# Self-attention in a decoder layer: the order of two DMA transposes in SyncE's queue

## The reference

```
q, k, v = x @ wq, x @ wk, x @ wv          # per head, 128 wide
qn, kn  = rms_norm(q) * q_scale, rms_norm(k) * k_scale
attn    = softmax(einsum('bqhd,bkhd->bhqk', qn, kn))
out     = einsum('bhqk,bkhd->bqhd', attn, v)
x       = x + einsum('bqhd,hde->bqe', out, wo)
```

## Time and profile before

| | us |
|---|---|
| median of 3 runs (lowest, highest) | 2565.74 (2563.83, 2566.78) |
| the profiled execution, its own time | 2562.61 |
| its span, first to last instruction | 2560.1 |
| PE busy in the span | 2459.1 |
| DVE, ACT, POOL busy | 1554.3, 1340.1, 844.0 |
| DMA transposes issued by SP | 252 |

### The profile page before, as it was taken

One profiled execution on the slowest core, in us unless ns is written; L12 is line 12 of the kernel. 1 busy time (PEld: TensorE's weight loads), 2 busy tenths in 40 slices (PEclk: granted clock), 3 DMA queues, 4 the chain that ended last, 5 costly groups with the idle time before them and its releaser, 6 DMA issues.

```text
span 2560.1 us, 46046 instructions
## 1 busy us (share of the span) xinstructions
PE 2459.1 (96%) x16474; PEld 1334.5 (52%) x16474; DVE 1554.3 (61%) x3592; ACT 1340.1 (52%) x4109; POOL 844.0 (33%) x794
## 2 busy tenths in 40 slices
PE   6998999999999999999888999999999999999998
PEld 3554554554554555544454465465465465465466
DVE  7777766666566666666545655655655655655644
ACT  4554555555555555565464563563563563564433
POOL 3333333333333333333222422422422422422412
PEclk9999999999999999999969999999999999999999
DMA  5677667777677767798611001001001001001000
GB/s 157 147 175 164 148 151 166 157 166 167 144 164 169 156 154 179 163 187 186 145 63 50 33 18 53 1 18 53 1 18 53 1 17 53 1 18 41 8 17 14
DMA packets 456259, 241.56 MB, mean 94 GB/s; under 512 B 389136, under 2 KB 391824, under 8 KB 455284
## 3 DMA queue, kind: packets, MB, share of 16 engines
q1 hardware_dynamic: 456034, 238.63, 39.8%
HBM read 78.66 MB, written 32.77 MB: 44 GB/s over the span
## 4 chain that ended last, share of the span: by engine, by line
PE 90%; DVE 4%; ACT 3%; issue 2%; POOL 1%; POOLq 0%; ACTq 0%; DVEq 0%
PE ps L1553 25%; PE ps L1555 24%; PE ps L1554 24%; PE ps L1732 3%; PE ps L1733 2%; PE ps L1734 2%; PE ps L1846 2%; ACT mem L974 2%; PE ps L1830 1%; PE ps L1802 1%; PE ps L1742 1%; PE ps L1746 1%; PE ps L1744 1%; PE ps L1824 1%; DVE mem L1224 1%
## 5 line engine op out<-in xcount | busy, mean ns | idle before, releaser
L1553 PE MATMUL ps<-mem 128*128 128x512 f16 (+7 forms) x3992 | 1226.8, 326 | 46.0 <-issue 30.3
L1554 PE MATMUL ps<-mem 128*128 128x512 f16 (+7 forms) x3992 | 1238.2, 325 | 0.0
L1555 PE MATMUL ps<-mem 128*128 128x512 f16 (+7 forms) x3992 | 1222.2, 325 | 0.0
L1553 PEld LDWEIGHTS ps<-mem 128*128 128x128 f16 (+3 forms) x3992 | 413.5, 104 | 372.4 <-issue 51.2
L1555 PEld LDWEIGHTS ps<-mem 128*128 128x128 f16 (+3 forms) x3992 | 414.7, 104 | 316.7 <-issue 9.0
L1554 PEld LDWEIGHTS ps<-mem 128*128 128x128 f16 (+3 forms) x3992 | 416.4, 104 | 305.0 <-issue 8.0
L749 POOL TENSOR_TENSOR mem<-mem 128x500 f32<-128x500 f32 (+1 forms) x231 | 269.2, 1165 | 460.6 <-DVE mem L1505 194.6
L699 POOL TENSOR_TENSOR mem<-mem 128x8 f32<-128x8 f32 x100 | 163.7, 1637 | 510.1 <-DVE mem L1137 510.1
L844 ACT ACTIVATE mem<-ps,mem 100x100 f32<-100x100 f32 x512 | 169.1, 346 | 186.4 <-DVE mem L1167 185.4
L1505 DVE TENSOR_TENSOR mem<-mem 128x500 f16<-128x500 f32 (+1 forms) x231 | 144.7, 650 | 177.0 <-ACT mem L1032 170.8
L711 POOL TENSOR_TENSOR mem<-mem 100x400 f16<-100x400 f32 x128 | 158.5, 1238 | 184.6 <-ACT mem L854 184.6
(11 more groups left out here) (123 smaller groups left out, 3045.5 us busy)
## 6 DMA issues: line engine op xcount, KB each, us to landing
x<-mem SPq DMA_DIRECT2D x100, 256.0 KB, 2.9
mem<-x SPq DMA_DIRECT2D x75, 256.0 KB, 3.7
mem<-in_x SPq DMA_DIRECT2D x50, 256.0 KB, 3.3
mem<-x SPq DMA_DIRECT2D x12, 1000.0 KB
mem<-mem SPq DMA_DIRECT2D x32, 200.0 KB
mem<-mem SPq DMA_DIRECT2D x6, 1000.0 KB
out<-mem SPq DMA_DIRECT2D x6, 1000.0 KB
mem<-in_wq SPq DMA_DIRECT2D x16, 256.0 KB, 4.1
```

The source lines that it names most:

```text
L1553: pe.matmul(out_ap, ah, bh, start=(i == 0), stop=False)
L1554: pe.matmul(out_ap, ah, bl, start=False, stop=False)
L1555: mm = pe.matmul(out_ap, al, bh, start=False, stop=(i == len(pairs) - 1))
```

## The change

In SP's loop over the steps the two calls change places: a step's tiles are turned first, and the probabilities of batch n + 1 after them. Nothing else differs: the same DMAs with the same waits, on the same queue.

```
                     load_rows(yn, rows_of(x1, 0, GB), GB, "yn_in")
                     load_keys(keys_of(0, GB), GB)
+                for u in projected_at(n - 1):
+                    turn_tile(u)
                 if 0 <= n + 1 < STEPS:
                     turn_probs(n + 1)
-                for u in projected_at(n - 1):
-                    turn_tile(u)
```

## The result

The changed kernel takes 2545.51 us (median of 4 runs, 2543.38 to 2549.29) where the kernel before takes 2566.26 (4 runs, 2563.83 to 2566.81): a ratio of 0.9929, 95% interval 0.9913 to 0.9944. That is 20.7 us less; forecast were 16.5 less, 2549.2. The two profiled executions of the changed kernel took 2549.29 and 2551.17 us, with spans of 2546.9 and 2549.4.

A forecast was written before the change was run, and what follows sets the result against it. PE bounds most of stage A, so only its 17.6 us idle could be won: 14.8 from waits plus 1.7 from clock, 16.5 us; 2562.6 became 2546.1, plus 3.1 gave 2549.2 us. Range 2543 to 2554, chance 0.70.

The forecast's parts named there:

- Step (1): On SP's queue, the tile issues at least 1.4 us earlier, and its landing moves by as much.
- the floor of 1.4: Least saving per tile in us: the other transpose's issue with its waits and small gaps; 1.43 in the step shown.
- rival A: The tile's transfer, not its issue, is the limit: gain only 9 us, time 2556 to 2557; chance 0.13.
- Step (2): Of PE's 15 waits before scores, 310 to 1240 us, eleven vanish and two leave 0.7 and 1.8: 14.8 us saved.
- Step (3): PE's waits before 310 and at 1248.44 us count at nothing; upper bound 6.8 us.
- Step (4): The granted clock, 0.91 between 1140 and 1160 us, no longer falls: 1.7 us more, between 0 and 1.8.
- (5): The probabilities leave later, behind a tile's issue of 4.24 or 5.65 us, but their cover suffices: cost 0.
- (6): SP's queue has the same work and reaches later DMAs earlier; its wait for `qlo` holds up nothing that could have gone.
- rival C: Probabilities become late behind the tile's transfer and hold ACT, kernel slower: 2575 us; chance 0.04.
- The offset: The 3.1 us by which before's median exceeded its profiled execution, added to 2546.1 to give 2549.2.
- Rival B: DVE and ACT chains are late next; if all is given back, 2563 to 2566 us, no change; chance 0.08.
- rival D: Waits outside the stretch and the 2.5 us forecast to stay also go: up to 26 us, 2540; chance 0.05.

The follow-up runs named there:

- e1: The changed kernel run once more with no edit, for a second profile: 2547.14 us, ratio 0.9943 to the kernel before.
- e3: Against the kernel before, only the 24 tiles turned twice go ahead of the probabilities, the others stay behind: 2552.75 us, ratio 0.9961.
- e4: Against the kernel before, only the 76 tiles turned once go ahead of the probabilities, double turns stay behind: 2559.64 us, ratio 0.9985.
- e7: Changed kernel, but of a double turn only the copy into the fifth slot precedes the probabilities, the other half follows, with its own semaphore: 2541.68 us, ratio 0.9910.
- e11: The kernel of e7 run once more, with no further edit: 2542.49 us, ratio 0.9914 to the kernel before.
- e2: Changed kernel, but SP again waits for `plo` and `o` before it turns a step's tile: 2554.49 us, ratio 0.9968 to the kernel before.
- e8: Changed kernel, but probabilities are turned behind `place_values`, the store and the residual rows of the next step: 2551.99 us, ratio 0.9951.
- e5: Changed kernel, but tiles are turned ahead of the store, residual rows and all loads, behind `place_values`: 2569.02 us, ratio 1.0016 to the kernel before.
- e6: Changed kernel, but tiles are turned before everything else of the step, `place_values` too: 2651.04 us, ratio 1.0344 to the kernel before.

## Why the prediction was right, and where it was not

**The mechanism: shown.** PE's waits for turned queries and keys were the only idle time of the stretch that mattered. Each ends 0.09 us after a tile's landing, and they shrank with the order (e1), by tile (e3, e4), and by halving the double turn (e7, e11).

**Step (1), "the landing moves by as much as the issue does": nearly right on the average, wrong where it mattered, by 1.05 us at the wait near 632.** Over the tiles turned between 310 and 1240 the issue comes 2.4 us earlier on the average after DVE L1162 has ended (0.4 us after it, before 2.8), and the landing 2.1 us earlier. So the issue gained more than the floor of 1.4, and most of that reached the landing. At the five tiles whose waits stayed the issue gained 1.35, 1.37, 1.36, 1.45 and 2.17 us, as forecast, and the landing only 0.30, 0.62, 0.70, 0.72 and 1.48. Two of them, as SP and PE have them in the changed kernel:

```profile
1135.65 4.94 SPq L583 DMA_TRANSPOSE mem<-mem  x1
...
1142.76 0.22 PE L1553 MATMUL ps<-mem 128*100 128x100 f16 x1 [2.42 <-issue]
...
1190.86 4.67 SPq L583 DMA_TRANSPOSE mem<-mem  x2
...
1199.40 0.22 PE L1553 MATMUL ps<-mem 128*100 128x100 f16 x1 [0.70 <-issue]
```

From issue to PE's start 7.11 and 8.54 us, where it was 1153.69 - 1147.32 = 6.37 and 1213.51 - 1205.65 = 7.86. Over the whole stretch the issue of L583 went from a middle of 2.23 us to 2.54, its landing from 4.5 to 4.8. This is rival A, at these tiles and not in general. Where SP comes to the tile at most 0.3 us after the end of its DMA before, which is so at 21 of 78 tiles, the first issue takes 3.3 us and its landing 5.6 on the average; where SP had stood waiting for more than 1 us, at 51, they take 2.2 and 4.8. That in the old order the tile's way was freer, by the time that SP had spent waiting and issuing the other transpose, fits this but is not shown: the transfers ahead and the length of the issue moved together, and no run separates them.

**Step (2), the sum.** Forecast to stay: 0.7 + 1.8 = 2.5 us at two waits. Measured: 6.1 at five, 1.89, 0.44, 0.65, 2.42 and 0.70. So 11.2 us of listed idle time went, not 14.8. The floor of 1.4 us was one for the issue, but not for the landing: two of the eleven short waits, 1.06 and 1.35 us, stayed in part.

**A term that was missing.** The listed idle time is too small. In the changed kernel the matmul at 629.94 is drawn 0.38 us long, but matmuls of this kind follow each other every 0.21 or 0.22 us (629.73, 629.94). The scores could have begun at 630.16, so the loss is 2.05 us, not the 1.89 in the brackets. By this a wait costs 0.16 us more than it shows; ten waits fewer make 1.6 us, an estimate from this one place. That pays for nearly half of the error in (2). With the 1.8 us of the clock, 11.2 + 1.6 + 1.8 = 14.6 us, and stage A of the first profile is 14.1 us shorter (1259.88 - 1245.78).

**Step (3), the waits outside count nothing: right,** to 0.2 us at each of the three places shown.

**Step (4), the clock: right in one profile and wrong in the other.** The granted clock between 1140 and 1160 was 1.00 in the first profile of the changed kernel:

```profile
1140.00:1160.00 20.00, 17.58 (x111) 8.74 (x110) 10.75 (x25) 9.73 (x31) 5.55 (x5) 1.00 1.03 224
```

and 0.91 in the second, with the same 2.4 us of wait. The threshold that I read from two rows (2.19 kept it, 3.30 did not) does not exist as such: in the second profile 2.1 us lowered it, and in e2's 2.35 us lowered it (0.91 from 620 to 640) while 2.75 us did not (1.00 from 1140 to 1160).

**Steps (5) and (6), the probabilities and SP's queue: right for the change itself.** The probabilities have a wide cover (e8). Behind SP's new waits at `klo` and `qlo` lay less cover than (6) made it seem: one place further ahead they held up loads and values (e5, e6). The landing of L602 kept its middle, 3.4 before and 3.3 us after. The Trainium skill, DMA: Bandwidth & Descriptors, section Queues, rings and completion order, has each DMA engine take descriptors in ring order. The trace agrees as far as it goes: for all 100 tiles the probabilities of the same step landed after the tile issued ahead of them, by 0.6 us at least, though their later issue alone may give that. And issued behind the tile, they landed as soon after their own issue as before; rival C did not come about.

**The offset.** I added 3.1 us because the median of before lay above its profiled execution. For the changed kernel it lies 3.8 us below. In the two profiled executions the gain is 2562.61 - 2549.29 = 13.3 us, in the medians 20.7 and, run again, 15.9. That 16.5 lies between them is in part luck: the sum of (2) was 3.6 us too large, a term was missing, and the offset had no ground. That the time fell 3.7 us beside 2549.2 owes as much to this as to any step. Rival B (something else late next) took nothing that is seen beside the 1.2 us at stage A's end; rival D would have needed the outer waits.

## What to carry to other kernels

In an in-order issue queue, rank the DMAs by how long after issue each is wanted, and read that margin from the trace for every one of them, the plain loads too: here some of the tiles had none, the probabilities most of a step, and values and weights so little that a further move cost 22 to 104 us. Look at the engine's waits too: what stands behind a wait is late by it. Where one DMA that is wanted early is two transfers, give the half that is wanted first a semaphore of its own. And count a wait from start to start of the matmuls around it, not only by the idle time that the profile lists.

## What was not expected of the hardware

One DMA transpose of 128 x 2048 two-byte elements held SP for 1.70 to 4.24 us before and 1.70 to 4.94 after, though nothing in its form differs. It took longer where SP came straight from another DMA (3.3 us against 2.2, see step (1)); why, no run shows. Issue and landing of the two lines in the changed kernel, 310 to 1240:

```profile
L583 SPq DMA_TRANSPOSE mem<-mem x97: 1699/2536/4937, 317.3 to 1227.7; - x97
DMA to landing us min/median/max: 4.3/4.8/7.0
```
```profile
L602 SPq DMA_TRANSPOSE mem<-mem x101: 1228/1310/7107, 309.3 to 1235.6; - x101
DMA to landing us min/median/max: 2.9/3.3/11.1
```

And waits of PE of the same length, 2.4 us at the same place of the same program, were followed by the lower of the two clock levels in one execution and not in another.
